# Four-layer graph network on one core: SyncE's order of network stores, loads and counted tiles in the counting stage, and paired first-layer products with four activation slots in the convolution

## The chip, the cores and the metric

The kernel runs on one core of one Trainium2 chip. The time is the device time in microseconds (us) of one execution. Before the change its median over three runs is 11267.62 us (11256.81 to 11269.58).

## The reference, cut to what matters

Four graph layers follow each other over 6250 nodes and 206250 edges sorted by destination; after each one the nodes are `x = layernorm(x + layer(x))`. Two parts of the reference bear on the change:

```python
# last layer: an edge network whose result needs the edge inputs only
w_ij = _mlp(edge_feats, rad_w0, rad_b0, rad_w1, rad_b1)
w_ij = w_ij + _mlp(chi_scalar, sph_w0, sph_b0, sph_w1, sph_b1)
...
# third layer (convolution), for every edge
h = jax.nn.silu(edge_scalars @ W_fc1 / np.sqrt(10.0))   # 10 numbers -> 100
w = h @ W_fc2 / np.sqrt(100.0)                          # 100 -> 4*32
x0e = y0[edge_src]
x1e = y1[edge_src]
...                                                     # messages of 256 numbers
sums = jax.ops.segment_sum(edge_feat, edge_dst, num_segments=n)
```

The first layer (attention over neighbours) and the second one (a mean over neighbours) are computed with a dense matrix of edge counts between nodes, which the kernel makes first.

## The kernel before, in words

The engines' programs are written by hand, each in its own block, with semaphores between them. Every engine works through its own instructions in order. A group is 512 edges (four tiles of 128); there are 404 groups.

**Counting** (`count_edges`, L324 to L410). 392 windows are counted, in 49 iterations of `VB` = 8 windows (index v). For each window VectorE builds 0/1 rows and columns (L256, L259), TensorE multiplies them (L293), ScalarE copies the counts out of PSUM (L318) and makes a mask (L321), VectorE measures a maximum with it (L280, two windows behind), and SyncE stores the counts to `c_dram` (L339). Counts have four slots in SBUF, so ScalarE may copy window k only when the store of window k-4 has landed.

Between the windows of this stage runs a part of the last layer's edge network (`EdgeMlp`), three groups ("units", `UB` = 3) to an iteration, in places fixed by the tables at the top of the kernel (`COUNT_PAIR0` and so on). TensorE makes the first products in pairs, on rows 0 to 63 and 64 to 127 of the array (L909), ScalarE applies SiLU (L929), TensorE makes the second product (L918), VectorE adds a bias and multiplies by a factor (L935, L938) into the single tile `mlp_w`, SyncE stores that tile to `w_dram` (L891) and loads the next features (L882). There is one `mlp_w`, so VectorE waits ahead of L935 until the store of the unit before has landed, and TensorE waits ahead of L918 until VectorE has done L938 of the unit before. VectorE runs `mlp.vector` behind the hots and the measure of windows v = 0, 4 and 6. SyncE is one queue: for each window it waits until ScalarE has copied the counts of that window (L338), then stores them, and then comes to the loads (v = 1, 4, 6) and to the stores of the network (v = 1, 5, 7).

**Convolution** (`conv_edges`, L1606 to L1791). 101 iterations of `S` = 4 groups (index s). For each group GpSimd gathers 4 x 128 rows of `y_dram` (L1708, four slots of rows), TensorE makes the first product of the network from ten scalars per edge (L1716, 10 rows of the array, PSUM slot g % 2), ScalarE applies SiLU (L1688, `hid`, two slots) and makes the 0/1 matrix of destinations (L726, L729), TensorE makes the second product (L1721, `w_ps`, two slots), VectorE computes the messages (L1757 to L1771) and adds the sums to the nodes (L741, L742, for two groups at a time), and TensorE sums the messages by destination (L753). TensorE's order at group g is: first product of g+2, second product of g+1, sums of g. ScalarE's order is: 0/1 matrix of g, then SiLU of g+2, which waits for the second product of g, since it writes the slot that this one reads. GpSimd may gather into a slot when L1764 has read its last contents.

The order of the work around the change in the lines themselves:

```python
sp.wait_ge(c.copied, k + 1)                                  # L338
sp.dma_start(c_dram[bass.ds(k * P, P), :], c.counts[:, v % 4])
...
pe.wait_ge(hid_done, g + 1)                                  # L1735
first(s % 2, (s + 2) % S, 16 * (i + 1 + (s >= S - 2)))
pe.wait_ge(msg_done, 1 + g)
second(g + 1, (s + 1) % 2)
pe.wait_ge(msg_done, 1 + g + 1)
lane_sums(nc, pe, c, s, g, 2 * i + s // 2, msgs[:, s])
```

Of the kernel before, what the change touches and what calls it, by code (L numbers as in the profile page):

```python
# [11 lines left out]
ACT = mybir.ActivationFunctionType  # L12
AX = mybir.AxisListType

P = 128
# [7 lines left out]
GE = T * P  # L23
S = 4
NI = -(-E // (S * GE))
# [298 lines left out]
def count_edges(nc, at, mlp, c_dram):  # L324


    with ExitStack() as st:
        c = EdgeCounts(nc, st)
        mlp.psum(nc, st, "count")
        with nc.Block() as block:  # L330

            @block.sync
            def _(sp):
                def body(i, first):
                    u = UB * i
                    for v in range(VB):
                        k = VB * i + v
                        sp.wait_ge(c.copied, k + 1)  # L338
                        sp.dma_start(c_dram[bass.ds(k * P, P), :], c.counts[:, v % 4]).then_inc(c.stored[v % 4], 16)  # L339
                        if v in (1, 4, 6):  # L340
                            mlp.load_next(sp, u + v // 2 - (v > 1))
                        if v == 1 and not first:
                            mlp.store(sp, u - 1)
                        if v in (5, 7):
                            mlp.store(sp, u + (v - 5) // 2)

                for s in range(4):
# [1258 lines left out]
def conv_edges(nc, shared, a, iota, spans, y_dram, acc):  # L1606


    with ExitStack() as st:
        sem = nc.alloc_semaphore  # L1610

        def sb(name, shape, dt=f32):
            return st.enter_context(nc.sbuf_tensor(f"conv_{name}", shape, dt))
# [1 line left out]
        c = LaneSums(nc, st, "conv", iota, spans, acc, 2 * D)  # L1615
        rows = sb("rows", [P, S, T, D])
        stage = sb("stage", [P, S, T], i32)
        scalars = sb("scalars", [10, S, GE])
        harm = sb("harm", [P, NT, 4])
        w1 = sb("w1", [10, 100])  # L1620
        w2 = sb("w2", [100, D])
        hid = sb("hid", [100, 2, GE])
        msgs = sb("msgs", [P, S, T, 2 * D])
        scaled = sb("scaled", [P, T, 2, MUL])
        t01 = sb("t01", [P, T, MUL])
# [4 lines left out]
        loaded = sem("conv_loaded")  # L1630
# [9 lines left out]
        scalars_in = [sem(f"conv_scalars_in{s}") for s in range(S)]  # L1640

        with nc.Block() as block:

            @block.sync
            def _(sp):
                for to, of in [(w1[:], a["L2_fc1"]), (w2[:], a["L2_fc2"]), (harm[:], a["harm"])]:
                    sp.dma_start(to, of).then_inc(loaded, 16)
                sp.wait_ge(loaded, 48)

            @block.vector  # L1650
            def _(dve):
                own = shared.own
                dve.wait_ge(loaded, 48)

                own.do(nc.vector.tensor_scalar(w2[:], w2[:], 0.1, None, ALU.mult))
                nc.vector.tensor_scalar(w2[:, 3 * MUL:], w2[:, 3 * MUL:], 3 ** -0.5, None, ALU.mult)

        with nc.Block() as block:

            @block.sync  # L1660
            def _(sp):
                def load_scalars(s, g):
                    sp.dma_start(scalars[:, s, :], a["scalars"][:, bass.ds(g * GE, GE)]).then_inc(scalars_in[s], 16)

                def load_indices(s, g):
# [4 lines left out]
                for s in range(S):  # L1670
                    load_scalars(s, s)
                with sp.Fori(0, NI) as i:
                    for s in range(S):

                        sp.wait_ge(gathered[s], 16 * T * (i + 1))
                        load_indices(s, S * (i + 1) + s)

                        sp.wait_ge(hid_sum, S * i + s + 1)
                        load_scalars(s, S * (i + 1) + s)
                for s in range(S):  # L1680
                    sp.wait_ge(scalars_in[s], 16 * (NI + 1))
                    sp.wait_ge(staged[s], 16 * (NI + 1))

            @block.scalar
            def _(act):
                def silu(g, n):
                    act.wait_ge(hid_sum, g + 1)
                    nc.scalar.activation(hid[:, n], hid_ps[0:100, n], ACT.Silu, scale=10 ** -0.5).then_inc(hid_done, 1)  # L1688

                silu(0, 0)  # L1690
                silu(1, 1)
                with act.Fori(0, NI) as i:
                    for s in range(S):
                        lane_hot(nc, act, c, s, S * i + s)

                        act.wait_ge(w_done, S * i + s + 1)
                        silu(S * i + s + 2, s % 2)

            @block.gpsimd
            def _(pool):  # L1700
# [10 lines left out]

            @block.tensor
            def _(pe):
                def first(n, slot, count):
                    pe.wait_ge(scalars_in[slot], count)
                    nc.tensor.matmul(hid_ps[0:100, n], w1[:], scalars[:, slot, :], start=True, stop=True).then_inc(hid_sum, 1)  # L1716

                def second(g, n):
                    pe.wait_ge(hid_done, g + 1)
                    for t in range(T):  # L1720
                        ins = nc.tensor.matmul(w_ps[:, n, t, :], hid[:, n, t * P:(t + 1) * P], w2[:], start=True, stop=True)  # L1721
                    ins.then_inc(w_done, 1)

                tensor_lane_start(pe, c)
                first(0, 0, 16)
                first(1, 1, 16)
                second(0, 0)
                with pe.Fori(0, NI) as i:
                    for s in range(S):
                        g = S * i + s  # L1730


                        pe.wait_ge(hid_done, g + 1)
                        first(s % 2, (s + 2) % S, 16 * (i + 1 + (s >= S - 2)))

                        pe.wait_ge(msg_done, 1 + g)
                        second(g + 1, (s + 1) % 2)
                        pe.wait_ge(msg_done, 1 + g + 1)
                        lane_sums(nc, pe, c, s, g, 2 * i + s // 2, msgs[:, s])
                        if s % 2 == 1:  # L1740
                            lane_sums_x(nc, pe, c, s, 2 * i + s // 2, lambda t: msgs[:, s - 1 + t // T, t % T])

            @block.vector
            def _(dve):
                def message(i, s):
# [9 lines left out]
                    dve.wait_ge(msg_done, 1 + g)  # L1755
                    dve.wait_ge(gathered[s], 16 * T * (i + 1))
                    own.mark(nc.vector.tensor_tensor(t11[:], y1, sh1, ALU.mult))  # L1757
                    dve.wait_ge(w_done, g + 1)
                    own.mark(nc.vector.tensor_tensor(scaled[:], w[:, :, 0:2], hs[:, :, 0:1].unsqueeze(3).to_broadcast([P, T, 2, MUL]), ALU.mult))
                    own.mark(nc.vector.tensor_tensor(t01[:], w[:, :, 2], y0, ALU.mult))  # L1760
                    own.wait_for(2)
# [389 lines left out]
```

## Time and profile before

| what | us |
|---|---|
| median of 3 runs | 11267.62 |
| the profiled execution, its own time | 11251.21 |
| its span, first to last instruction | 11249.4 |
| counting stage, 49 iterations | about 197 to 2370 of the span |
| dense stages of the first two layers | 2370 to 5300 |
| convolution, 101 iterations | 5300 to 8010 |
| last layer | 8010 to 11249 |

Shares of the whole span: TensorE's matmuls 73%, its weight loads 55% (beside the matmuls), VectorE 57%, ScalarE 44%, GpSimd 28%. The mean granted TensorE clock is 0.828 of full speed. Times in a timeline are microseconds from the start of the span; a wait is given as [idle time before, and what ended it]. The releaser "remote" is an event that the profile could not tie to an instruction, and "issue" is time in which the engine waited for nothing that the profile shows. Where a helper records the instructions, the line is that of the helper.

### The profile page before, as it was taken

Reading aid. Unit: us, or ns where it says so; the run is one execution under the profiler, and the core shown is the slowest. Engines: PE = TensorE matmul, PEld = TensorE weight load, DVE = VectorE, ACT = ScalarE, POOL = GpSimd, SP = SyncE. Lnnn points to the kernel's source line nnn. Section 1 sums busy time; section 2 is a strip of 40 time slices with the busy share of each in tenths; the row PEclk is TensorE's granted clock in tenths of the full one; section 3 lists DMA queues with packets and bytes.
Section 4 is the critical chain, followed back from the end, with each engine's and each line's share of the span. In section 5 each row is a group of like instructions: output and inputs, shape, how many; then the busy total and the mean of one; then the engine's idle time right before and its main releaser. Section 6 shows DMA issues by size and latency. Waiting matters only on the chain. (4 is left out here: it accounts for less than half of the span.)

```text
span 11249.4 us, 197335 instructions
## 1 busy us (share of the span) xinstructions
PE 8246.0 (73%) x51344; PEld 6196.6 (55%) x51345; DVE 6369.1 (57%) x11872; ACT 4935.1 (44%) x9054; POOL 3183.7 (28%) x3246
## 2 busy tenths in 40 slices
PE   3888888878869999994777777777657565656654
PEld 2555555567757777773555554554435454444443
DVE  5777777789943333335555555555655555555555
ACT  2444444468745555552333333333434333333332
POOL 0000000000000000000555555555235555555554
PEclk9889888899989999996777777777778777777776
DMA  2222222256623333331111111111045445454544
GB/s 80 104 104 104 103 105 102 104 174 227 213 92 122 119 122 123 118 105 31 43 43 43 43 43 43 43 43 43 19 133 149 143 142 143 143 145 141 143 144 115
DMA packets 634626, 1180.46 MB, mean 105 GB/s; under 512 B 215640, under 2 KB 295818, under 8 KB 615011
## 3 DMA queue, kind: packets, MB, share of 16 engines
q1 hardware_dynamic: 505288, 861.87, 24.0%
q0 software_dynamic: 129280, 317.93, 10.0%
q8 instruction: 24, 0.39, 0.0%
q14 instruction: 34, 0.28, 0.0%
HBM read 902.78 MB, written 276.57 MB: 105 GB/s over the span
## 5 line engine op out<-in xcount | busy, mean ns | idle before, releaser
L1708 POOL DMA_INDIRECT conv_rows<-y_dram,conv_stage x1616 | 1550.8, 960 | 4064.3 <-issue 3399.5
L1917 POOL DMA_INDIRECT att_kv_rows<-kv_dram,att_stage x1616 | 1625.4, 1006 | 1563.0 <-DVE att_msgs L2047 845.6
L753 PE MATMUL conv_part<-conv_msgs,conv_hot 128*128 128x256 f32 x3232 | 1060.2, 486 | 159.3 <-DVE conv_msgs L1771 115.0
L929 ACT ACTIVATE late_hid<-att_mlp,late_b 128x512 f32<-128x512 f32 x440 | 282.2, 684 | 1789.3 <-remote 821.0
L1688 ACT ACTIVATE conv_hid<-conv_hid_ps 100x512 f32<-100x512 f32 x406 | 240.2, 592 | 1731.1 <-remote 866.4
L1076 DVE SCALAR_TENSOR_TENSOR mean_rest<-mean_counts,mean_high 128x896 f16<-128x896 f32 x343 | 374.7, 1093 | 1077.7 <-ACT mean_high L1037 1077.7
L1721 PEld LDWEIGHTS conv_w_ps<-conv_w,conv_hid 100*128 100x128 f32 x3240 | 509.9, 240 | 831.8 <-ACT conv_hid L1688 549.3
L918 PE MATMUL att_mlp<-late_w,late_hid 128*128 128x128 f32 x3520 | 583.0, 334 | 504.2 <-ACT late_hid L929 457.8
L753 PEld LDWEIGHTS conv_part<-conv_msgs,conv_hot 128*128 128x128 f32 x3232 | 765.3, 249 | 321.7 <-DVE conv_msgs L1771 118.1
L1721 PE MATMUL conv_w_ps<-conv_w,conv_hid 100*128 100x128 f32 x3240 | 602.4, 343 | 461.9 <-ACT conv_hid L1688 448.2
L293 PE MATMUL count_ps<-count_cols,count_rows 128*128 128x392 bf16 x3920 | 802.8, 354 | 159.2 <-DVE count_cols L259 158.3
L918 PEld LDWEIGHTS att_mlp<-late_w,late_hid 128*128 128x128 f32 x3520 | 547.8, 245 | 530.2 <-ACT late_hid L929 478.8
L2044 DVE TENSOR_TENSOR att_qk<-att_q_ps,att_qk 128x512 f32<-128x512 f32 x404 | 279.5, 692 | 950.9 <-DMA conv_scalars<-in_scalars 805.5
L753 PE MATMUL att_part<-att_msgs,att_hot 128*128 128x128 f32 x3232 | 577.9, 334 | 324.1 <-DVE att_msgs L2047 251.9
L918 PE MATMUL count_mlp<-mlp_w,mlp_hid 128*128 128x128 f32 x4704 | 691.0, 315 | 142.5 <-DVE mlp_w L938 140.5
L918 PEld LDWEIGHTS count_mlp<-mlp_w,mlp_hid 128*128 128x128 f32 x4704 | 678.9, 230 | 189.4 <-issue 166.3
L1123 PE MATMUL mean_sum_ps<-wh,mean_turned 128*128 128x129 f32 x4802 | 696.5, 285 | 51.9 <-ACT mean_turned L1045 51.3
L293 PEld LDWEIGHTS count_ps<-count_cols,count_rows 128*128 128x128 bf16 x3920 | 380.1, 103 | 642.2 <-issue 449.1
L318 ACT ACTIVATE count_counts<-count_ps 128x784 f32<-128x784 f32 x392 | 322.7, 823 | 864.6 <-PE count_ps L293 857.8
L753 PEld LDWEIGHTS att_part<-att_msgs,att_hot 128*128 128x128 f32 x3232 | 501.5, 237 | 364.0 <-issue 198.4
L259 DVE TENSOR_SCALAR count_cols<-cols,col_key 128x784 bf16<-128x784 f16 x1960 | 687.0, 419 | 0.0
L577 PE MATMUL soft_ps<-wh,soft_weights 128*128 (+1 forms) x4802 | 579.9, 280 | 142.7 <-DVE soft_weights L521 142.7
(278 smaller groups left out, 16499.4 us busy)
## 6 DMA issues: line engine op xcount, KB each, us to landing
c_dram<-count_counts SPq DMA_DIRECT2D x392, 392.0 KB, 2.4
mean_counts<-c_dram SPq DMA_DIRECT2D x343, 448.0 KB, 3.6
att_w_rows<-w_dram SPq DMA_DIRECT2D x404, 256.0 KB
soft_counts<-c_dram SPq DMA_DIRECT2D x98, 1024.0 KB, 4.8
w_dram<-mlp_w SPq DMA_DIRECT2D x294, 256.0 KB, 2.5
mlp_feats<-in_feats SPq DMA_DIRECT2D x295, 192.0 KB, 2.7
soft_counts<-c_dram SPq DMA_DIRECT2D x49, 1088.0 KB, 5.0
att_lanes<-lo_dram SPq DMA_DIRECT2D x404, 128.0 KB
```

The lines of the kernel that those rows point to most:

```text
L259: ins = nc.vector.tensor_scalar(c.cols[:, b, t], at.cols[:], at.col_key[:, bass.ds(first + t, 1)], None, ALU.is_equal)
L293: ins = nc.tensor.matmul(c.ps[:, b, h, 0:CW // 2], rows, cols[:, h * (CW // 2):(h + 1) * (CW // 2)], start=first, stop=last)
L318: nc.scalar.activation(c.counts[:, v % 4].rearrange("p (h c) -> p h c", h=2), ps, ACT.Copy).then_inc(c.copied, 1)
L577: ins = nc.tensor.matmul(place(m), weights[:, b, m * P:(m + 1) * P], win(wh, w), start=False, stop=False, skip_group_check=True)
L753: ins = nc.tensor.matmul(part, c.hot[:, s, t, :], rows[:, t, :], start=half == 0 and t == 0, stop=half == 1 and t == T - 1)
L918: ins = nc.tensor.matmul(self.w_ps[:, t * D:(t + 1) * D], self.hid[:, n, t * P:(t + 1) * P], self.w1[:, n, :], start=n == 0, stop=n == 2 * ...
L929: nc.scalar.activation(self.hid[:, n], self.hid_ps[:, n % 2], ACT.Silu, bias=self.b0[:, n:n + 1]).then_inc(self.hid_done, 1)
L1076: nc.vector.scalar_tensor_tensor(rest[:, m], counts[:, m], 0.25, high[:, m], ALU.mult, ALU.subtract).then_inc(rest_done, 1)
L1123: ins = nc.tensor.matmul(sum_ps[:, 0:D + 1], turned[:, h, at:at + P], x_ext[:, k, :], start=k == 0, stop=k == NW - 1)
L1708: pool.indirect_dma_start(rows[:, s, t, :], None, y_dram, bass.IndirectOffsetOnAxis(ap=stage[:, s, t:t + 1], axis=0)).then_inc(gathered[s] ...
L1721: ins = nc.tensor.matmul(w_ps[:, n, t, :], hid[:, n, t * P:(t + 1) * P], w2[:], start=True, stop=True)
L1917: pool.indirect_dma_start(kv_rows[:, s, t, :], None, kv_dram, bass.IndirectOffsetOnAxis(ap=stage[:, s, t:t + 1], axis=0)).then_inc(gathere ...
```

## The change

In the counting stage SyncE's stores of the edge network's tile and its loads of the next features come ahead of its wait for the window's copied counts, and the stores move from the steps v = 1, 5, 7 to v = 0, 4, 6. VectorE's, ScalarE's and TensorE's programs of that stage stay as they are.

In the convolution the ten scalars of two groups are loaded to partitions 0 to 9 and 64 to 73 of one slot (`scalars` has two slots of pairs), the first-layer weight lies on both sets of rows, and TensorE makes the first products of groups g+2 and g+3 one behind the other when s is even. `hid` has four slots, so SiLU waits for the second product of two groups earlier; ScalarE does two SiLUs at even s. SyncE loads two scalars' rows at odd s.

```diff
                     for v in range(VB):
                         k = VB * i + v
+                        if v == 0 and not first:
+                            mlp.store(sp, u - 1)
+                        if v in (4, 6):
+                            mlp.store(sp, u + v // 2 - 2)
+                        if v in (1, 4, 6):
+                            mlp.load_next(sp, u + v // 2 - (v > 1))
                         sp.wait_ge(c.copied, k + 1)
                         sp.dma_start(c_dram[bass.ds(k * P, P), :], c.counts[:, v % 4]).then_inc(c.stored[v % 4], 16)
-                        if v in (1, 4, 6):
-                            mlp.load_next(sp, u + v // 2 - (v > 1))
-                        if v == 1 and not first:
-                            mlp.store(sp, u - 1)
-                        if v in (5, 7):
-                            mlp.store(sp, u + (v - 5) // 2)
...
-        scalars = sb("scalars", [10, S, GE])
+        scalars = sb("scalars", [P, 2, GE])
-        w1 = sb("w1", [10, 100])
+        w1 = sb("w1", [P, 100])
-        hid = sb("hid", [100, 2, GE])
+        hid = sb("hid", [100, S, GE])
...
+        def rows_of(n):
+            return slice(n * P // 2, n * P // 2 + 10)
...
-                def load_scalars(s, g):
-                    sp.dma_start(scalars[:, s, :], a["scalars"][:, bass.ds(g * GE, GE)]).then_inc(scalars_in[s], 16)
+                def load_scalars(p, g):
+                    for n in range(2):
+                        sp.dma_start(scalars[rows_of(n), p, :], a["scalars"][:, bass.ds((g + n) * GE, GE)]).then_inc(scalars_in[p], 16)
...
-                        sp.wait_ge(hid_sum, S * i + s + 1)
-                        load_scalars(s, S * (i + 1) + s)
+                        if s % 2 == 1:
+                            sp.wait_ge(hid_sum, S * i + s + 1)
+                            load_scalars(s // 2, S * (i + 1) + s - 1)
...
                         lane_hot(nc, act, c, s, S * i + s)
-                        act.wait_ge(w_done, S * i + s + 1)
-                        silu(S * i + s + 2, s % 2)
+                        if s % 2 == 0:
+                            for n in range(2):
+                                act.wait_ge(w_done, S * i + s + n + 1)
+                                silu(S * i + s + 2 + n, (s + 2 + n) % S)
...
+                pe.sem_inc(w_done, 2)
...
-                        pe.wait_ge(hid_done, g + 1)
-                        first(s % 2, (s + 2) % S, 16 * (i + 1 + (s >= S - 2)))
+                        if s % 2 == 0:
+                            pe.wait_ge(hid_done, g + 2)
+                            first((s // 2 + 1) % 2, i + 1 + (s >= S - 2))
                         pe.wait_ge(msg_done, 1 + g)
-                        second(g + 1, (s + 1) % 2)
+                        second(g + 1, (s + 1) % S)
...
-                    dve.wait_ge(w_done, g + 1)
+                    dve.wait_ge(w_done, 2 + g + 1)
```

## Rows read from the trace of the kernel before

**Rows 1.** Busy time by stage: counting, convolution; us, engines, granted clock, DMA, GB/s.
```profile
190.00:2370.00 2180.00, 1773.49 (x9914) 1151.93 (x9914) 1586.67 (x3645) 1051.50 (x1421) 0.37 (x1) 0.89 0.28 103
5300.00:8010.00 2710.00, 2076.36 (x7284) 1369.16 (x7284) 1367.63 (x3638) 955.08 (x2427) 1550.80 (x1616) 0.75 0.18 43
```
**Rows 2.** Waits in the counting stage: total us, times, longest.
```profile
DVE mlp_w L935 <- DMA w_dram<-mlp_w: 435.1, 96, 7.4
...
PE count_ps L293 <- DVE count_cols L259: 156.7, 52, 3.2
PE count_mlp L918 <- DVE mlp_w L938: 140.5, 49, 2.9
...
PE count_mlp L909 <- ACT mlp_hid L929: 62.5, 46, 1.5
...
PE count_mlp L909 <- DMA mlp_feats<-in_feats: 31.6, 50, 1.5
```
**Rows 3.** The same stage, SyncE's own waits.
```profile
SPq L339 <- ACT count_counts L318: 1751.2, 391, 10.3
```
**Rows 4.** Timeline of counting, steps v = 4 to 7 of one iteration.
```profile
1225.64 0.69 DVE L938 TENSOR_TENSOR mlp_w<-mlp_w,mlp_cut 128x512 f32<-128x512 f32 x1
...
1228.52 3.84 PE L918 MATMUL count_mlp<-mlp_w,mlp_hid 128*128 128x128 f32 x32
...
1232.35 0.96 DVE L280 CUSTOM_DVE_ANT_0 count_shifted<-s_rows,count_gaps 128x784 f32<-128x784 f32 x1
...
1235.70 1.13 PE L909 MATMUL count_mlp<-mlp_feats,mlp_w 64*128 64x512 f32 x4
1235.81 0.82 ACT L318 ACTIVATE count_counts<-count_ps 128x784 f32<-128x784 f32 x1 [0.51 <-PE count_ps L293]
...
1237.32 0.33 SPq L891 DMA_DIRECT2D w_dram<-mlp_w  x1
...
1239.83 0.69 DVE L935 TENSOR_TENSOR mlp_w<-count_mlp,mlp_b 128x512 f32<-128x512 f32 x1 [6.51 <-DMA w_dram<-mlp_w]
...
1241.51 4.77 PE L918 MATMUL count_mlp<-mlp_w,mlp_hid 128*128 128x128 f32 x26 [2.92 <-DVE mlp_w L938]
```
**Rows 5.** DMA issues: KB each, median us from issue to landing.
```profile
w_dram<-mlp_w SPq DMA_DIRECT2D x294, 256.0 KB, 2.5
```
**Rows 6.** Waits in the convolution: total us, times, longest.
```profile
ACT conv_hid L1688 <- remote: 866.4, 97, 22.9
POOL conv_rows L1708 <- DVE conv_msgs L1764: 664.9, 178, 6.0
```
**Rows 7.** Groups of instructions: GpSimd's gathers and TensorE's first products.
```profile
L1708 POOL DMA_INDIRECT conv_rows<-y_dram,conv_stage x1616 | 1550.8, 960 | 4064.3 <-issue 3399.5 <-DVE conv_msgs L1764 664.9
L1716 PE MATMUL conv_hid_ps<-conv_scalars,conv_w 10*100 10x512 f32 x812 | 508.1, 708 | 29.3 <-DMA conv_scalars<-in_scalars 29.3
```
**Rows 8.** Timeline of the convolution around one gap of all engines.
```profile
6510.05 1.10 PE L1716 MATMUL conv_hid_ps<-conv_scalars,conv_w 10*100 10x512 f32 x2
...
6512.10 0.94 POOL L1708 DMA_INDIRECT conv_rows<-y_dram,conv_stage  x1 [0.30 <-issue]
6515.34 0.60 ACT L1688 ACTIVATE conv_hid<-conv_hid_ps 100x512 f32<-100x512 f32 x1 [9.43 <-remote]
...
6515.59 0.48 DVE L741 SCALAR_TENSOR_TENSOR acc<-conv_part,span_upper,acc 128x256 f32 x1 [8.44 <-remote]
...
6518.92 1.00 POOL L1708 DMA_INDIRECT conv_rows<-y_dram,conv_stage  x1 [5.88 <-DVE conv_msgs L1764]
```
**Rows 9.** Timeline of the convolution: TensorE at half clock, and a short wait of GpSimd.
```profile
6536.56 2.08 PE L1721 MATMUL conv_w_ps<-conv_w,conv_hid 100*128 100x128 f32 x8 [4.70 <-ACT conv_hid L1688]
...
6542.41 2.02 PE L1716 MATMUL conv_hid_ps<-conv_scalars,conv_w 10*100 10x512 f32 x2
...
6544.36 2.08 PE L1721 MATMUL conv_w_ps<-conv_w,conv_hid 100*128 100x128 f32 x8
...
6548.65 1.00 POOL L1708 DMA_INDIRECT conv_rows<-y_dram,conv_stage  x1 [0.73 <-DVE conv_msgs L1764]
```

More of the change, by code:

```diff
@@ L1639, in conv_edges @@
         gathered = [sem(f"conv_gathered{s}") for s in range(S)]
-        scalars_in = [sem(f"conv_scalars_in{s}") for s in range(S)]
+        scalars_in = [sem(f"conv_scalars_in{p}") for p in range(2)]
+        def rows_of(n):
+            return slice(n * P // 2, n * P // 2 + 10)
         with nc.Block() as block:
@@ L1645, in _ @@
             def _(sp):
-                for to, of in [(w1[:], a["L2_fc1"]), (w2[:], a["L2_fc2"]), (harm[:], a["harm"])]:
+                for to, of in [(w1[rows_of(0)], a["L2_fc1"]), (w1[rows_of(1)], a["L2_fc1"]), (w2[:], a["L2_fc2"]), (harm[:], a["harm"])]:
                     sp.dma_start(to, of).then_inc(loaded, 16)
-                sp.wait_ge(loaded, 48)
+                sp.wait_ge(loaded, 64)
             @block.vector
@@ L1652, in _ @@
                 own = shared.own
-                dve.wait_ge(loaded, 48)
+                dve.wait_ge(loaded, 64)
                 own.do(nc.vector.tensor_scalar(w2[:], w2[:], 0.1, None, ALU.mult))
@@ L1669, in _ @@
                     load_indices(s, s)
-                for s in range(S):
-                    load_scalars(s, s)
+                for p in range(2):
+                    load_scalars(p, 2 * p)
                 with sp.Fori(0, NI) as i:
@@ L1676, in _ @@
                         load_indices(s, S * (i + 1) + s)
-                        sp.wait_ge(hid_sum, S * i + s + 1)
-                        load_scalars(s, S * (i + 1) + s)
+                        if s % 2 == 1:
+                            sp.wait_ge(hid_sum, S * i + s + 1)
+                            load_scalars(s // 2, S * (i + 1) + s - 1)
+                for p in range(2):
+                    sp.wait_ge(scalars_in[p], 32 * (NI + 1))
                 for s in range(S):
-                    sp.wait_ge(scalars_in[s], 16 * (NI + 1))
                     sp.wait_ge(staged[s], 16 * (NI + 1))
@@ L1685, in _, with silu @@
             def _(act):
-                def silu(g, n):
+                def silu(g, s):
                     act.wait_ge(hid_sum, g + 1)
-                    nc.scalar.activation(hid[:, n], hid_ps[0:100, n], ACT.Silu, scale=10 ** -0.5).then_inc(hid_done, 1)
+                    nc.scalar.activation(hid[:, s], hid_ps[0:100, s % 2], ACT.Silu, scale=10 ** -0.5).then_inc(hid_done, 1)
                 silu(0, 0)
@@ L1713, in _, with first, second @@
             def _(pe):
[L1714 to L1718, printed above, removed]
+                def first(p, count):
+                    pe.wait_ge(scalars_in[p], 32 * count)
+                    for n in range(2):
+                        nc.tensor.matmul(hid_ps[0:100, n], w1[rows_of(n)], scalars[rows_of(n), p, :], start=True, stop=True).then_inc(hid_sum, 1)
+                def second(g, s):
                     pe.wait_ge(hid_done, g + 1)
                     for t in range(T):
-                        ins = nc.tensor.matmul(w_ps[:, n, t, :], hid[:, n, t * P:(t + 1) * P], w2[:], start=True, stop=True)
+                        ins = nc.tensor.matmul(w_ps[:, s % 2, t, :], hid[:, s, t * P:(t + 1) * P], w2[:], start=True, stop=True)
                     ins.then_inc(w_done, 1)
                 tensor_lane_start(pe, c)
-                first(0, 0, 16)
-                first(1, 1, 16)
+                pe.sem_inc(w_done, 2)
+                first(0, 1)
                 second(0, 0)
```

## The prediction, made before the changed kernel was run

> **What bounds the kernel now.** I read the busy time by stage first. The two stages touched are counting, some 2175 us up to 2370 or 44.4 us for each of its 49 iterations, and the convolution, 2710 us or 6.7 us for each of 404 groups [rows 1]. In counting TensorE is busy 81% and VectorE 73%, so neither is obviously the bound; in the convolution they are at 77% and 50%, with the clock at 0.75. Busy shares don't say what a change is worth, so the waits come next.
>
> In counting VectorE's one large wait is for the store of the network's tile to land: 435.1 us in 96 waits, two for each iteration [rows 2]. The page has VectorE busy 1587 us there, so without this wait its chain would be 2180 - 435 = 1745 us, of which some 160 us are short gaps with no other engine behind them. TensorE's waits are 156.7 us for VectorE's columns, 140.5 for L938, 62.5 for ScalarE's SiLU and 31.6 for the features: 391 us [rows 2]. The first two are the store's wait once more, handed on: L918 waits for L938 of the unit before.
>
> The timeline shows why the store lands late [rows 4]. L938 of a unit is through at 1226.3. SyncE issues its store at 1237.32, 11 us later, because it stands behind the wait for copied counts of window v = 5, whose copy starts at 1235.81. The store needs 2.5 us [rows 5], and L935 starts at 1239.83 after 6.51 us of idleness, though TensorE's products for it (L918, from 1228.52 for 3.84) were there at 1232.4. TensorE then waits 2.92 at 1241.51. SyncE is idle for 1751 us in that wait [rows 3]: the queue has time, it only stands in the wrong order.
>
> In the convolution every third group ends in a gap in which TensorE, ScalarE and VectorE all stand: TensorE's last product starts at 6510.05, yet ScalarE's SiLU and VectorE's addition come at 6515.34 and 6515.59, released within 0.3 us of each other, 2.3 us after GpSimd has ended a run of gathers (6512.10 + 0.94) [rows 8]. The next such gap stands ahead of 6536.56 [rows 9], 21 us or three groups on. GpSimd itself waits 5.88 us until a message frees rows. It waits 664.9 us in all [rows 6]; its gathers take 0.960 + 0.30 us each, 1616 of them, 2036 us [rows 7]. So this stage is GpSimd's run of 12 gathers (15.1 us), a gap of 4 to 6, and again.
>
> **The change, part by part.**
>
> *Counting, the order on SyncE.* The stores go from behind the copies of v = 5, 7 and 1 to ahead of those of v = 4, 6 and 0. The store of the unit finished at 1226.3 can then be issued right behind the counts of v = 3, at about 1227, and lands at 1229.5. L935 may start when VectorE is through with its measure (1232.35 + 0.96 = 1233.3) and L918 is done (1232.4): at 1233.4 in place of 1239.83. The other wait of the iteration goes the same way, its store being issued a copied window earlier. Removed: up to the 435 us.
>
> What is late next? VectorE's chain is then 1745 us, 35.6 an iteration. TensorE's 2180 less its 391 of waits is 1789, but these contain stretches at half clock (mean 0.89); the ScalarE wait of 62.5 may stay. TensorE and VectorE come so near to each other that they will take turns in waiting for single windows: hots of v = 7 need the sums of v = 5, which come behind 32 of L918 and a pair. I take 0.8 us an iteration for it, 40 us, as L909's wait for ScalarE (62.5 / 49 = 1.3) is the nearest row. Gain 435 - 40 = **395 us**. Bounds: 435, and below 300, if TensorE keeps all but its two waits for VectorE (156.7 + 140.5 = 297).
>
> *What the moved steps may hold up.* SyncE's queue now waits for L938 of v = 4 ahead of the copied counts of v = 4. VectorE ends the network's step behind the hots and a measure of v = 4, TensorE's sums of v = 4 and the copy come later, so the counts' store isn't late; with four slots it could be by windows. The loads of features wait for TensorE's second pair of the same step, which stands ahead of its sums. Cost nothing, hidden in the 1751 us; without this cover, the delay of a store by one L935 and L938, 1.5 us, 49 times, 75 us at most. The features' wait of 31.6 shrinks with it. c_dram's and w_dram's bytes are the same.
>
> *Convolution, the pairs.* Two products for one time: the network in counting does four matmul instructions of 64 rows and 512 columns in 1.13 us (the x4 row) [rows 4], where two instructions of 10 rows take 1.10 here at full clock and 2.02 at half [rows 8, 9]. That a pair on 10 rows of each half runs side by side as one on 64 does isn't in the trace; between no overlap (gain 0; a loss is excluded, since two in line are what stands now) and all (one product in two), I take all, that pair being the nearest row. It saves 0.5 us a group at full and 1.0 at half clock, 400 groups: 200 to 400 us of TensorE. Little of it is on the path: the cycle is set by GpSimd's run and the gap behind it, and three groups pass in it. What it shortens is the third message, which now and then makes GpSimd wait 0.73 us between gathers [rows 9]; of its 664.9 us I put the 134 long gaps (404 / 3) at 4.7 us, 630, which leaves 35. Gain from that: 30.
>
> *Four activation slots.* ScalarE no longer waits for the product of its own group, so in half of the gaps TensorE has one more second product done when the semaphores come. The next message is then ready at once, and sometimes a fourth group gets into a cycle. Each cycle less saves about 4.7 us. I take few, 4 of 134: 20 us. Bounds: 0, and a fourth in every cycle, 134 - 101 = 33 cycles, 155 us.
>
> *SyncE in the convolution.* 404 loads of scalars stay 404, two behind each other at odd s. The load now waits for the gathers of one group later than before, but those are ahead of that group's message, and the pair is used behind that message's sums. One more load of w1 at the start, 0.3 us of issue. Together nothing.
>
> **Sum.** Profiled execution 11251.2 - 395 - 50 = 10806 us. The median of the runs stood 16 above that execution, so **10823 us**.
>
> **Rivals.**
>
> 1. *TensorE becomes the bound of counting.* For: 81% busy, and its pieces are uneven. Against: its waits of 391 go at the same time. Gain there 297: 10921.
>
> 2. *The convolution is TensorE's after all.* For: it is the busiest engine. Against: the gaps end with GpSimd's runs. If its time counts, half of the 508 us of first products [rows 7] goes, 254 in place of 50: 10619.
>
> 3. *Slower: only two groups to a cycle in the convolution.* If the pair makes the third group's second product late, GpSimd gets rows for 8 gathers and then stands the longest gap, 10.1 + 6.0 = 16.1 us for two groups, 8.05 against 6.7 each: +545 us. With the gain of counting: 11251 - 395 + 545 + 16 = 11417. It decides when this product ends later than before; at half clock first and second product and sums take 7.8 us a group (6536.56 to 6544.36) [rows 9], and the pair has the length of one product, so I see no reason.
>
> 4. *The clock.* In the convolution it is at 0.75 of full, falling in the gaps [rows 1, 8]; with less work TensorE idles more. At half clock throughout, a group takes 7.8 - 1.0 = 6.8 us of TensorE against 6.7 now, +40 us in place of -50: 10913. The Trainium skill, TensorE: Matmul & The Clock Gate, section HAM oscillation, says that idle gaps between bursts bring the clock down to half: by that rule this rival gets likelier, and the gain in counting too, where the gaps close. The trace agrees for counting, with 0.89 at 81% busy.
>
> 5. *The store's wait doesn't go, or another takes its place* (feature loads late, SyncE held up): gain 0 to 75 in counting, 50 in the convolution: 11142 to 11217.
>
> **How the numbers follow.** A measurement of this kernel can tell 0.2% from no change, 23 us. The forecast has 0.56, rival 1 0.12, rival 2 0.12, rival 3 0.02, rival 4 0.10, rival 5 0.08, of which 0.03 would show no difference and 0.01 a loss. The range reaches from just above rival 2 (its low end, with 435 in counting, lies below), 10640, to beyond rivals 1 and 4 together (11251 - 297 + 40 + 16 = 11010), 10990. Faster 0.94, same 0.03, slower 0.03.
>
> **What would show it.** In the profile after: the wait of L935 for w_dram nearly gone; counting 36.4 us an iteration, ending near 1980; VectorE's share there near 0.89, the clock above 0.93; SyncE's store of the tile issued within 2 us of L938. In the convolution: four instructions of L1716 in about 1.1 us at full clock, GpSimd's waits near 615 us, its gathers unchanged, the stage near 2660 us. I'd be wrong if L935 waits as long for something else, if TensorE's waits in counting don't fall, if the convolution moves by more than 150 us, or if GpSimd's runs become shorter than 12 gathers.

## The result, and the profile after

| | before, us | changed, us | ratio |
|---|---|---|---|
| median (4 runs each) | 11265.78 (11256.81 to 11269.58) | 10849.32 (10845.47 to 10860.84) | 0.9633 [0.9616, 0.965] |
| profiled execution | 11251.21 | 10860.84 | |
| counting, L293's first to last product | 2164.6 | 1734.7 | |
| convolution, first to last gather | 2681.3 | 2676.9 | |
| last layer, first to last gather | 2934.3 | 2974.4 | |

The change makes the kernel faster by 3.7%; 10823 us were forecast, with a range of 10640 to 10990. The execution that was profiled after is the slowest of its four. In the traces counting gives 430 us, the convolution 4, and the last layer, which the change doesn't touch, takes 40 back. In that layer GpSimd's wait for free rows grew by as much, from 845.6 to 886.3 us.

Busy time by stage, after the change (the columns of [rows 1]):

```profile
190.00:1935.00 1745.00, 1596.31 (x9910) 1007.76 (x9910) 1576.68 (x3639) 1053.25 (x1421) 0.00 (x0) 0.98 0.35 129
4880.00:7580.00 2700.00, 1851.64 (x7284) 1344.18 (x7284) 1362.37 (x3639) 947.11 (x2427) 1552.13 (x1616) 0.74 0.18 43
```

In counting VectorE's work is the same to 10 us, 1577 of now 1745, or 90%. TensorE's fell from 1773 to 1596 though its instructions are the same ones: the granted clock of the stage went from 0.89 to 0.98, with less idle time between its products. In the convolution TensorE's work fell by 225 us and the stage did not.

The waits in the counting stage after the change, first those of TensorE and VectorE, then SyncE's (the columns of [rows 2, 3]):

```profile
PE count_ps L293 <- DVE count_cols L259: 74.2, 79, 3.2
...
DVE count_rows L256 <- PE count_ps L293: 69.8, 93, 1.7
...
PE count_mlp L909 <- ACT mlp_hid L929: 62.0, 46, 1.5
...
DVE count_rows L256 <- issue: 55.7, 143, 1.5
...
SPq L345 <- ACT count_counts L318: 1199.9, 377, 8.8
SPq L891 <- DVE mlp_w L938: 125.7, 130, 4.7
```

Of [rows 2] L935's 435.1 us for `w_dram`, L918's 140.5 for L938 and the 31.6 for the features have no row any more. L293's wait for columns is halved, L909's wait for SiLU is as it was. VectorE's wait for TensorE's sums has grown to 69.8 us, and its short gaps ahead of L256 with no releaser have shrunk to 55.7. Before they were:

```profile
DVE count_rows L256 <- issue: 102.7, 206, 1.5
...
DVE count_rows L256 <- PE count_ps L293: 5.3, 7, 1.4
```

SyncE now waits 125.7 us for L938, ahead of the copied counts; ScalarE has no wait for a counts slot to be stored, so no delay of anybody shows.

The timeline at the same time of the span, which is some five iterations further on; the three units shown are those of the steps v = 6, 0 and 4 (against [rows 4], where L938 at 1225.64 is of v = 4):

```profile
1211.87 0.69 DVE L935 TENSOR_TENSOR mlp_w<-count_mlp,mlp_b 128x512 f32<-128x512 f32 x1
...
1212.71 0.69 DVE L938 TENSOR_TENSOR mlp_w<-mlp_w,mlp_cut 128x512 f32<-128x512 f32 x1
...
1213.57 0.33 SPq L891 DMA_DIRECT2D w_dram<-mlp_w  x1
...
1214.48 3.84 PE L918 MATMUL count_mlp<-mlp_w,mlp_hid 128*128 128x128 f32 x32
...
1221.88 0.69 DVE L935 TENSOR_TENSOR mlp_w<-count_mlp,mlp_b 128x512 f32<-128x512 f32 x1
...
1238.97 0.69 DVE L938 TENSOR_TENSOR mlp_w<-mlp_w,mlp_cut 128x512 f32<-128x512 f32 x1
...
1239.83 0.33 SPq L891 DMA_DIRECT2D w_dram<-mlp_w  x1
```

The store goes out 0.2 us after L938 ends (1213.40 to 1213.57, 1239.66 to 1239.83), where it was 11 us behind. The L935 at 1221.88 comes 8 us after the store ahead of it, without an idle time. The page's median from issue to landing is 2.0 us for these stores (2.5 in [rows 5]).

GpSimd's gathers and TensorE's first products over the whole run, and two waits of the convolution:

```profile
L1717 POOL DMA_INDIRECT conv_rows<-y_dram,conv_stage x1616 | 1552.1, 960 | 4071.2 <-issue 3418.2 <-DVE conv_msgs L1774 652.9
L1726 PE MATMUL conv_hid_ps<-conv_scalars,conv_w 10*100 10x512 f32 x812 | 270.0, 745 | 32.2 <-DMA conv_scalars<-in_scalars 32.2
```
```profile
ACT conv_hid L1695 <- remote: 1086.2, 99, 21.5
POOL conv_rows L1717 <- DVE conv_msgs L1774: 652.9, 172, 6.2
```

The first products cost 270.0 us in place of the 508.1 of [rows 7]: they do run side by side. GpSimd's wait for rows is 652.9, from 664.9: the gaps in which all stand are still there, and so the 238 us of TensorE bought nothing here.

### The profile page after: what moved, and what is told of

The parts are those of the page before. It is cut to its first block and busy times, and to the rows that moved or that the text cites. A ratio compares the mean times of both kernels' runs of the same rounds, so it can differ in the third digit from the quotient of the medians.

```text
span 10859.0 us, 197378 instructions
## 1 busy us (share of the span) xinstructions
PE 7869.4 (72%) x51344; PEld 6050.9 (56%) x51345; DVE 6358.3 (59%) x11872; ACT 4929.6 (45%) x9054; POOL 3189.9 (29%) x3246
## 5 line engine op out<-in xcount | busy, mean ns | idle before, releaser
L1927 POOL DMA_INDIRECT att_kv_rows<-kv_dram,att_stage x1616 | 1630.2, 1009 | 1595.6 <-DVE att_msgs L2057 886.3
L753 PE MATMUL conv_part<-conv_msgs,conv_hot 128*128 128x256 f32 x3232 | 1091.5, 497 | 451.4 <-DVE conv_msgs L1781 345.9
L918 PE MATMUL att_mlp<-late_w,late_hid 128*128 128x128 f32 x3520 | 591.7, 335 | 496.7 <-ACT late_hid L929 427.2
L918 PEld LDWEIGHTS att_mlp<-late_w,late_hid 128*128 128x128 f32 x3520 | 555.3, 247 | 524.6 <-ACT late_hid L929 447.0
L293 PE MATMUL count_ps<-count_cols,count_rows 128*128 128x392 bf16 x3920 | 747.2, 336 | 75.7 <-DVE count_cols L259 74.2
L293 PEld LDWEIGHTS count_ps<-count_cols,count_rows 128*128 128x128 bf16 x3920 | 363.6, 99 | 533.8 <-issue 237.0
L577 PEld LDWEIGHTS soft_ps<-wh,soft_weights 128*128 128x128 f32 x4802 | 553.2, 194 | 169.9 <-issue 167.2
L1123 PEld LDWEIGHTS mean_sum_ps<-wh,mean_turned 128*128 128x128 f32 x4802 | 590.4, 191 | 70.8 <-DVE acc L1080 57.8
L1937 PEld LDWEIGHTS att_q_ps<-att_q_both,att_hot_t 128*128 128x128 bf16 x4848 | 365.1, 114 | 472.5 <-issue 388.1
```

Of the source, the lines that this page charges most:

```text
L293: ins = nc.tensor.matmul(c.ps[:, b, h, 0:CW // 2], rows, cols[:, h * (CW // 2):(h + 1) * (CW // 2)], start=first, stop=last)
L577: ins = nc.tensor.matmul(place(m), weights[:, b, m * P:(m + 1) * P], win(wh, w), start=False, stop=False, skip_group_check=True)
L753: ins = nc.tensor.matmul(part, c.hot[:, s, t, :], rows[:, t, :], start=half == 0 and t == 0, stop=half == 1 and t == T - 1)
L918: ins = nc.tensor.matmul(self.w_ps[:, t * D:(t + 1) * D], self.hid[:, n, t * P:(t + 1) * P], self.w1[:, n, :], start=n == 0, stop=n == 2 * ...
L1123: ins = nc.tensor.matmul(sum_ps[:, 0:D + 1], turned[:, h, at:at + P], x_ext[:, k, :], start=k == 0, stop=k == NW - 1)
L1927: pool.indirect_dma_start(kv_rows[:, s, t, :], None, kv_dram, bass.IndirectOffsetOnAxis(ap=stage[:, s, t:t + 1], axis=0)).then_inc(gathere ...
```

## The experiments

Three sets were run, each on a chip of its own and beside the kernel before on the same chip. So each set has its own time of before: 11245.59 us (11229.46 to 11259.53), 11254.23 us (11250.29 to 11264.15) and 10029.41 us (10010.06 to 10035.85). The third chip comes up again below.

### First set: which part carries what

**The order on SyncE alone**, with the convolution of before (the first hunk of the diff and nothing else).

> SyncE's new order in counting alone, convolution as before. Theory: the change's gain is all here, since VectorE's wait of 435.1 us for the landed tile (rows 2) is gone: counting ends about 430 us earlier (the products of counting end near 1929 us in place of 2358), time 10835 to 10860, 0.962 to 0.964 of before. Rival: the convolution's pairs carry a part of it; then this one gains under 380 us and stands above 10890.

**The convolution alone**, with SyncE's old order.

> The convolution's pairs and four slots alone, SyncE's order in counting as before. Theory: GpSimd's runs of gathers and the gaps behind them set the stage, so the paired products give little: the stage from the first to the last gather goes from 2681 to about 2677 us, and the time is within 20 us of before, ratio 0.998 to 1.001. Rival (TensorE's work counts): 250 us less, ratio 0.978. Second rival: the pairs make what follows slower, the last layer by some 40 us as in the profile of the changed kernel: ratio 1.003.

**The stores alone**: they move ahead of the wait as in the change, the loads stay behind the counts' store.

```diff
+                        if v == 0 and not first:
+                            mlp.store(sp, u - 1)
+                        if v in (4, 6):
+                            mlp.store(sp, u + v // 2 - 2)
                         sp.wait_ge(c.copied, k + 1)
                         sp.dma_start(c_dram[bass.ds(k * P, P), :], c.counts[:, v % 4]).then_inc(c.stored[v % 4], 16)
                         if v in (1, 4, 6):
                             mlp.load_next(sp, u + v // 2 - (v > 1))
-                        if v == 1 and not first:
-                            mlp.store(sp, u - 1)
-                        if v in (5, 7):
-                            mlp.store(sp, u + (v - 5) // 2)
```

> Of SyncE's new order only the stores of the network's tile move ahead of the wait for copied counts; the loads of features stay behind it; convolution as before. Theory: the stores carry the gain, at least 400 of 430 us, and the rest is TensorE's wait for features, 31.6 us before (rows 2), which may grow, since TensorE now comes to the pairs earlier: time 10850 to 10890. Rival: with TensorE faster, the late loads become the new wait, one landing of 2.7 us an iteration and the wait for the copy ahead of it, some 150 us lost: near 11000.

**The loads alone**: they go ahead of the wait, the stores stay where they were.

```diff
+                        if v in (1, 4, 6):
+                            mlp.load_next(sp, u + v // 2 - (v > 1))
                         sp.wait_ge(c.copied, k + 1)
                         sp.dma_start(c_dram[bass.ds(k * P, P), :], c.counts[:, v % 4]).then_inc(c.stored[v % 4], 16)
-                        if v in (1, 4, 6):
-                            mlp.load_next(sp, u + v // 2 - (v > 1))
```

> Of SyncE's new order only the loads of features move ahead; the stores stay late. Theory: VectorE's wait of 435 us stays, and at most TensorE's 31.6 us for features go, most of it hidden behind VectorE: 0 to 30 us, ratio 0.997 to 1.000. Rival: the loads matter as much as the stores: a gain of over 100 us.

| kernel | median, us | ratio to before | counting | convolution | last layer |
|---|---|---|---|---|---|
| order on SyncE | 10802.77 | 0.9605 [0.959, 0.962] | 1735.3 | 2685.4 | 2911.2 |
| convolution | 11175.26 | 0.994 [0.9926, 0.9954] | 2166.8 | 2604.3 | 2921.0 |
| stores alone | 10810.27 | 0.9611 [0.9595, 0.9627] | 1744.9 | 2683.6 | 2928.0 |
| loads alone | 11199.58 | 0.9959 [0.9943, 0.9974] | 2119.7 | 2685.7 | 2925.8 |

The three stages are read from the traces as in the first table. The order alone came out 32 us below its forecast of 10835 to 10860 us, and the convolution alone, forecast at 0.998 to 1.001, at 0.994. The stores alone came out 40 us below their 10850 to 10890. They carry counting: 420 of its 430 us. Alone, the loads give 45, more than the features' wait of 31.6 and than the 0 to 30 expected; together with the stores only some 10 are left. That the two waits lie partly in the same stretch would explain it, but is not shown. The waits of the counting stage with the loads alone say the same:

```profile
DVE mlp_w L935 <- DMA w_dram<-mlp_w: 399.3, 96, 6.8
PE count_ps L293 <- DVE count_cols L259: 159.9, 55, 3.2
PE count_mlp L918 <- DVE mlp_w L938: 153.6, 49, 3.3
```

The features have no row, L935 has lost 36 of its 435 us, and all that hangs on the store stands. The convolution alone gives 70 us by the medians, and its stage is 81 us shorter than with the order on SyncE alone: a gain that the first comparison did not show. So either the parts don't add up, or the first comparison was an odd one.

### Second set: what in the convolution gives the gain

**The changed kernel once more**, without an edit.

> The changed kernel once more, beside its parts on one chip. In the other job counting alone gave 0.9605 of before and the convolution's part alone 0.994, where the changed kernel's own runs gave 0.9633. Theory: the parts add up on one and the same chip, 0.9605 x 0.994 = 0.955, and the 0.9633 was that chip's. Rival: the parts don't add up, and pairs behind the shorter counting are worth nothing or a loss: 0.960 to 0.964 again, with the stage of the gathers near 2677 us and the last layer's gathers near 2974.

**Four slots only**: counting as changed, four slots of `hid` and the later wait of SiLU, but single first products in the old order.

```diff
-        hid = sb("hid", [100, 2, GE])
+        hid = sb("hid", [100, S, GE])
...
-                        silu(S * i + s + 2, s % 2)
+                        silu(S * i + s + 2, (s + 2) % S)
...
-                        second(g + 1, (s + 1) % 2)
+                        second(g + 1, (s + 1) % S)
```

> Counting as changed; in the convolution four activation slots, but single first products in the order of before. Theory: TensorE's own work is not on the path, the held-back SiLU is: the slots bring what the convolution's part brings, stage of the gathers 2604 to 2640 us. Rival: the shorter work of the pairs brings it, and this one stays at 2685 us, 0.9605 of before.

**Pairs with two slots**: the changed kernel, but `hid` with two slots, so that SiLU waits for the product of its own slot as before.

```diff
-        hid = sb("hid", [100, S, GE])
+        hid = sb("hid", [100, 2, GE])
...
-                                act.wait_ge(w_done, S * i + s + n + 1)
+                                act.wait_ge(w_done, 2 + S * i + s + n + 1)
```

> The changed kernel with two activation slots in place of four: SiLU of the second group of a pair waits for the second product of the group just before it. Theory of the slots: the gain of the convolution is gone, gathers' stage 2685 us or more. Theory of TensorE's work: unchanged against the changed kernel, within 10 us.

**Pairs in line**: the changed kernel, but both products of a pair on rows 0 to 9, so that they can't run side by side.

```diff
-        scalars = sb("scalars", [P, 2, GE])
+        scalars = sb("scalars", [10, 2, 2, GE])
...
-                        nc.tensor.matmul(hid_ps[0:100, n], w1[rows_of(n)], scalars[rows_of(n), p, :], start=True, stop=True).then_inc(hid_sum, 1)
+                        nc.tensor.matmul(hid_ps[0:100, n], w1[rows_of(0)], scalars[:, p, n, :], start=True, stop=True).then_inc(hid_sum, 1)
```

> The changed kernel with both products of a pair on rows 0 to 9, so that they can't run side by side; order and slots as changed. If TensorE's saved time (0.5 us a group at full clock, 1.0 at half) is worth nothing, the time is that of the changed kernel within 15 us; if it is on the path, it is 100 to 300 us longer.

| kernel | median, us | ratio to before | convolution | last layer |
|---|---|---|---|---|
| changed, again | 10755.74 | 0.9556 [0.9543, 0.9569] | 2618.4 | 2929.8 |
| four slots only | 10817.05 | 0.9613 [0.9599, 0.9626] | 2682.0 | 2916.7 |
| pairs, two slots | 10743.79 | 0.9543 [0.953, 0.9556] | 2610.8 | 2922.5 |
| pairs in line | 10734.12 | 0.9543 [0.953, 0.9556] | 2601.8 | 2917.4 |

The parts do add up: 0.9605 times 0.994 is 0.9547, and the changed kernel is at 0.9556. It was the first comparison that had little from the convolution. Four slots alone are worth nothing against the order on SyncE alone (0.9613 against 0.9605). Two slots do as well as four (12 us less in the medians), and in line does as well as side by side (22 us less, where 15 either way were allowed for). What the kernels with the gain of 64 to 80 us have in common is the **order**: two first products one behind the other at every second group, with the two SiLUs and the loads that go with them. Each of my two reasons was taken away with the other in place, and the gain stayed, so neither is needed by itself. That both can go at once is not shown: the kernel without both (third set) ran only on a chip without these gaps.

GpSimd's waits for rows show it, here the four-slot kernel, the changed one again, and the pairs in line (convolution):

```profile
POOL conv_rows L1708 <- DVE conv_msgs L1765: 659.2, 167, 6.0
```
```profile
POOL conv_rows L1717 <- DVE conv_msgs L1774: 601.3, 182, 6.0
```
```profile
POOL conv_rows L1717 <- DVE conv_msgs L1774: 566.6, 176, 5.9
```

The idle stretches of over 2 us between GpSimd's gathers, counted in the traces, show what the order changes. With single first products (before, order on SyncE, stores alone, loads alone, four slots only) there are 133 or 134, of 4.8 to 4.9 us in the mean, and at most 9 of the runs between them have fewer than 12 gathers. With products in twos (changed again, two slots, in line, convolution alone) there are 142 to 156, of 3.7 to 4.0 us, and 29 to 69 runs have fewer than 12, nearly all of them 8. So the gaps come more often and are shorter. In the first trace of the changed kernel they came as often (145, with 36 short runs), but took 4.4 us each: that is why its stage gained 4 us only.

The stages stand in the same order, 2682, 2618 and 2602, and TensorE's busy time does not: it is 1834 us side by side and 1981 in line (1993 with the 61 products that fall behind the window's end).

```profile
4880.00:7525.00 2645.00, 1834.32 (x7284) 1334.76 (x7284) 1361.74 (x3639) 947.10 (x2427) 1551.57 (x1616) 0.75 0.18 44
```
```profile
4880.00:7487.00 2607.00, 1980.66 (x7223) 1370.34 (x7224) 1352.87 (x3611) 954.42 (x2411) 1555.48 (x1616) 0.76 0.18 44
```

The timeline of the changed kernel, run again, around one gap:

```profile
6516.07 0.95 POOL L1717 DMA_INDIRECT conv_rows<-y_dram,conv_stage  x1 [0.30 <-issue]
...
6516.10 1.10 PE L1726 MATMUL conv_hid_ps<-conv_scalars,conv_w 10*100 10x512 f32 x4
...
6518.61 0.27 PE L1731 MATMUL conv_w_ps<-conv_w,conv_hid 100*128 100x128 f32 x1 [0.43 <-issue]
6518.91 0.43 DVE L1769 TENSOR_TENSOR conv_scaled<-conv_w_ps,conv_harm 128x256 f32<-128x256 f32 x1 [5.43 <-remote]
6518.95 1.09 ACT L1695 ACTIVATE conv_hid<-conv_hid_ps 100x512 f32<-100x512 f32 x2 [6.35 <-remote]
6520.98 1.00 POOL L1717 DMA_INDIRECT conv_rows<-y_dram,conv_stage  x1 [3.97 <-DVE conv_msgs L1774]
...
6523.56 0.42 DVE L1769 TENSOR_TENSOR conv_scaled<-conv_w_ps,conv_harm 128x256 f32<-128x256 f32 x1
```

Four instructions take the 1.10 us of two. SiLU (both of the pair) and the next message start 0.04 us apart, 1.9 us after GpSimd's last gather has ended (6516.07 + 0.95 = 6517.02), as in [rows 8] (2.3 us there). But the message was not held up here: the second product that it reads ended only at 6518.88 (6518.61 + 0.27), 0.03 us ahead of the message. GpSimd's gap is 3.97 us, where [rows 8] has 5.88. One gap proves nothing of the sum, but it is the kind of difference that the waits add up.

### Third set: what ends the gaps

Two theories stood: that the signals of TensorE reach the others only when GpSimd pauses (then more pauses would help), and that a pause of GpSimd is simply lost time.

**No gathers.** It leaves GpSimd's gathers of the convolution out (the rows are set to 1 once), so the stage shows what the other engines need by themselves.

```diff
-                        for t in range(T):
-                            pool.indirect_dma_start(
-                                rows[:, s, t, :], None, y_dram,
-                                bass.IndirectOffsetOnAxis(ap=stage[:, s, t:t + 1], axis=0)).then_inc(gathered[s], 16)
+                        pool.sem_inc(gathered[s], 16 * T)
```

> The changed kernel with the convolution's gathers left out: rows are set to 1 once, GpSimd only raises the semaphores. Theory: the gaps in which TensorE, ScalarE and VectorE all stand come from GpSimd's long runs of gathers (TensorE's semaphores arrive some 2 us after a run ends); without them the gaps go and the stage is bound by TensorE or VectorE, 4 to 4.6 us a group, 1620 to 1860 us in place of 2620 to 2680. Rival: the gaps are TensorE's own, from its clock or its queue; then they stay, and the stage takes over 2300 us.

**A pause after every second group**: GpSimd waits for its own gathers to land. **A pause after every group** does the same for each.

```diff
                             pool.indirect_dma_start(
                                 rows[:, s, t, :], None, y_dram,
                                 bass.IndirectOffsetOnAxis(ap=stage[:, s, t:t + 1], axis=0)).then_inc(gathered[s], 16)
+                        if s % 2 == 1:
+                            pool.wait_ge(gathered[s], 16 * T * (i + 1))
```

> The changed kernel; in the convolution GpSimd waits after every second group until the rows it has just gathered have landed. Theory (TensorE's semaphores are held while GpSimd issues a long run): a run is 8 gathers, 10.1 us, and 2 us of pause, about 6.05 us a group in place of 6.5, the stage of the gathers near 2450 us, 150 us faster than the changed kernel. Rival: the pause is only time lost on the busiest queue, 2 us for two groups on top, 200 us slower.

> As pause2, but GpSimd waits after every group: 5.0 us of gathers and 2 of pause, 7.0 us a group by GpSimd alone, stage near 2830 us, if nothing else holds. By the theory of held semaphores TensorE is never late then, the gaps of all three engines are gone, and the time is GpSimd's: 2830 us. By the rival it is 2620 plus 404 times 2, over 3300 us.

**Pairs in line with two slots**: both reductions of the second set together.

> Counting as changed; in the convolution only TensorE's and ScalarE's order changes: two first products one behind the other at even s, both on rows 0 to 9, and two activation slots. If the order alone carries the convolution's gain, it stands within 15 us of the kernels with pairs (0.954 to 0.956); if slots and overlap are each enough by themselves but not dispensable together, near 0.9605.

| kernel | time, us | ratio to before | convolution | last layer |
|---|---|---|---|---|
| no gathers | 9008.82 (one run) | | 1563.4 | 2251.5 |
| pause, every second group | 10047.52 | 1.002 [1.001, 1.0029] | 2605.6 | 2233.0 |
| pause, every group | 10406.3 (one run) | | 2968.5 | 2243.0 |
| pairs in line, two slots | 9595.23 | 0.9569 [0.9556, 0.9582] | 2157.3 | 2237.1 |

On this chip the kernel before takes 10029 us, 11% less than on the others. The last layer, with the same instructions, takes 2233 to 2252 us in place of 2911 to 2974. The gaps of all engines are gone in the convolution. The windows, VectorE's one large wait, and a stretch of GpSimd, of the pairs in line with two slots:

```profile
4880.00:7045.00 2165.00, 1854.66 (x7281) 1290.42 (x7282) 1367.73 (x3634) 967.75 (x2426) 1663.74 (x1616) 0.86 0.22 53
```
```profile
DVE conv_t L1767 <- DMA conv_rows<-y_dram,conv_stage: 607.2, 400, 9.7
```
```profile
6001.08 0.94 POOL L1717 DMA_INDIRECT conv_rows<-y_dram,conv_stage  x1 [0.30 <-issue]
6002.33 1.30 POOL L1717 DMA_INDIRECT conv_rows<-y_dram,conv_stage  x1 [0.30 <-issue]
6003.94 0.95 POOL L1717 DMA_INDIRECT conv_rows<-y_dram,conv_stage  x1 [0.30 <-issue]
```

GpSimd is without a wait for rows, and everybody waits for its gathers: 1616 of them at (1663.74 / 1616 =) 1.03 plus 0.30 us are 2149 us, and the stage is 2157. Here the convolution is bound by GpSimd's issue alone, and nothing that TensorE does can help; so this kernel's 0.9569 says nothing on whether the order carries the gain where there are gaps. The total agrees: 10029 - 9595 = 434 us, which is counting's gain with nothing beside it. A pause every second group costs (2605.6 - 2157.3) / 202 = 2.2 us, one every group (2968.5 - 2157.3) / 404 = 2.0 us, both against the pairs in line with two slots, as the changed kernel itself did not run on this chip: here a pause is lost time. The stage of the second, 2968.5 us, fits neither of its forecasts, 2830 and over 3300. Neither the theory of held signals nor that of long runs of gathers was put to the test, since the chip shows no gaps that a pause, or leaving the gathers out, could shorten. Without the gathers the stage takes 1563 us from the first to the last message, 3.87 a group, at full clock:

```profile
4880.00:6450.00 1570.00, 1367.01 (x7281) 1027.62 (x7282) 1340.78 (x3633) 944.11 (x2426) 0.00 (x0) 1.00 0.04 6
```

So at full clock the other engines' own work is far from being the bound of the stage; what it would take at the 0.74 to 0.76 of the kernels with gaps no run shows. There the stage is, within 20 us, GpSimd's issue, 2036 us by [rows 7], and its waits for rows, 567 to 665 us in the rows above and [rows 6]. The pairs in line, with 159 us more of TensorE's work and no longer a stage, say that this work isn't what fills those waits.

## Why the prediction was right, and where its steps were not

**The total, 10823 us against 10849: in part luck.** Counting gave 35 us more than its term and the convolution 46 less in the traces compared, and the last layer took 40 that no term foresaw. The profiled executions are 55 us off (10806 against 10861). The medians are only 26 apart, since the execution profiled after stood 12 us above its median, where 16 below had been carried over.

**Counting, -395: the mechanism right, the term 35 us too small.** The store of the tile behind the wait for copied counts was the cost. It goes out 0.2 us after L938, L935's wait is gone, and the stores alone bring 420 us. I had put 36.4 us an iteration; it is 1734.7 / 49 = 35.4, close to the 35.6 of VectorE's chain without its wait. The 40 us that I took off for a new coupling were too much: VectorE does now wait 69.8 us for TensorE's sums, where it waited 5.3, but its short gaps ahead of L256 with no releaser fell from 102.7 to 55.7 us and its busy time by 10, so about 8 us are left as the price of the coupling. TensorE, the other candidate, was no limit: its busy time fell by 177 us at the higher clock. That the store's landing time would stay 2.5 us was a little high too (2.0).

**What the moved steps hold up, 0: right.** SyncE's 125.7 us ahead of the copied counts turn up in nobody's waits. The loads were worth 45 us by themselves, more than their own wait, and 10 behind the stores.

**Convolution, -50: the size near, the reasons wrong.** It was 4 us in the first pair of traces, but 60 to 80 us in two sets of runs, and 0, by the total, on the chip where GpSimd binds. The first reason was that the shorter pair ends GpSimd's short waits (30 us): the overlap is real (508 us of first products became 267 to 270, and 472 in line), but pairs in line gain as much. The second was that four slots give a ready product in half of the gaps (20 us): four slots alone gain nothing, and two slots with pairs gain all of it. Nor do cycles get fewer, as that term had it: 133 long gaps became 145. The step that failed is that I gave two edits a price each and none to the third thing in the same hunk, the order: first products now come at every second group, and the odd groups have none between them. With it the gaps are more and shorter, and their sum is 10% less (643 us before, 577 in the changed kernel run again). Why is not shown, and the order was not tried with both other things gone where there are gaps. Nor is it shown why the first changed run had neither this gain nor the last layer's 2930 us; whatever differed between those occasions is as large as this term. One of the signs of being wrong did come, the runs shorter than 12 gathers: 36 of 146 in the first changed trace, where the trace before has 6 of 134.

**Rival 1**, TensorE as the bound of counting: no, TensorE is busy 91% there, but the stage came out at VectorE's chain. **Rival 2**, the convolution as TensorE's: no; in line it works 159 us more and the stage isn't longer. **Rival 3**, two groups a cycle: a quarter of the cycles became such, but with shorter gaps and not with the longest, and no stage of over 3200 us came. **Rival 4**, the clock: in the convolution it stayed at 0.74 to 0.76, and a loss didn't come. The half about counting came true, 0.89 to 0.98 with the gaps closed. The Trainium skill, TensorE: Matmul & The Clock Gate, section HAM oscillation, has gaps between bursts bring the clock down, and these rows agree with it. **Rival 5**, the store's wait stays or another comes: no. The range was meant to reach beyond rivals 1 and 4 together, but its end, 10990, lies below their 11010.

## What to carry to other kernels

When one queue waits for events in program order, look for the item that is ready long before the event ahead of it: here a store stood 11 us behind a wait that had nothing to do with it, and moving it gave 420 us without touching any engine's work. An engine's saved time is worth what the stage's bound gives back: 240 us of TensorE off the path were worth nothing of their own, while the convolution gained 64 to 80 us just as well with its first products in line. And undo each thing that a hunk does by itself, its order among them, before giving the credit to one.

## What the runs showed of the hardware that was not expected

- The same kernel of before takes 11246 to 11266 us in the first comparison and the first two sets, and 10029 on the chip of the third. Each set was run once, so that it is the chip and not the occasion is not shown. In the traces the difference is in the two stages with GpSimd's gathers (convolution 2602 to 2686 against 2157 us, last layer 2911 to 2974 against 2233 to 2252); counting with the new order is 1734 to 1735 us on both. Of the kernel before there is no trace from the chip of the third set.
- On the slower ones ScalarE and VectorE start again together some 2 us after GpSimd has ended a run of gathers, and the profile names "remote" as the releaser (866 to 1191 us of SiLU's waits). In the trace of before SiLU's waits of this kind that are over 3 us end 2.15 us after the last gather in the median, and 4.0 us after TensorE's last first product. On the fast chip there is no such row. What holds them up is open.
- Products of 10 rows each, on the rows from 0 and from 64 of TensorE, run side by side: four instructions of 512 columns in 1.10 us at full clock, where two took 1.10 [rows 8].
